# Two attention-and-feed-forward layers on one core: the quantised feed-forward's steps, the key loads and one bias moved to other places of their queues

## The chip, the cores and the metric

The kernel runs on one core of one Trainium2 chip. The core has four compute engines that each run their own queue in order: PE (matrix products), ACT (activations and copies with a scale), DVE (vector work), POOL (more vector work), and SP, a queue that only issues transfers (DMAs) between HBM and on-chip memory. Engines wait for one another by semaphores. The metric is the device time of one execution in microseconds; smaller is better.

## The reference: two layers over 32 batches

`x` is (32, 256, 256): 32 batches of 256 rows. `ctx_768` is (32, 77, 192). Each layer is an attention block and a feed-forward block, both with a residual and a layer norm on what they read:

```
x = x + L0_xattn(layernorm(x), ctx)      16 heads of 64: q = xn@Wq, k = ctx@Wk, v = ctx@Wv
x = x + L0_ffn(layernorm(x))             silu(x@wg.T) * (x@wu.T), then @wd.T, int weights / 127
x = x + L1_xattn(layernorm(x), ctx)      softmax(q k^T / 8) v @ Wo + bo
x = x + L1_ffn(layernorm(x)):
    lhs_scale = max|row| / 127 ; q_lhs = clip(round(x / lhs_scale), -127, 127)
    q_rhs the same by column of rhs ; out = (q_lhs @ q_rhs) * lhs_scale * rhs_scale
```

The feed-forward of layer 1 is thus a rounding to whole numbers, one 256 x 256 product and a scaling; that of layer 0 has three larger products.

## The kernel before

A first part computes keys and values of all batches and both layers into HBM (`keys_d`, `vals_d`) and prepares the weights. Then one long pipeline runs over h = 0 to 65: h counts batches, 0 to 31 of layer 0 and 32 to 63 of layer 1, and the last two drain. Within h there are four slots, u = 0 to 3, of four heads each, a *unit*. `lay[d]` is the layer of batch h + d, so `lay[-1] == 1` holds where the attention of batch h - 1 belongs to layer 1. Batches 4 to 28 and 36 to 60 run in hardware loops with one body each; each engine's `body` writes out, slot by slot, the order of its own queue. The order is by hand; nothing schedules it.

What a unit k = 4h + u does in its life:

- PE: `scores` (query times key) for two halves of 128 rows, t = 0 and 1, from key buffer `kb[u // 2]` (L957). One PSUM area holds them, so the scores of unit k wait for the exponentials of k - 1.
- DVE takes the maxima (L1288), ACT the exponentials with their sums (L1137), DVE the reciprocals (L1293).
- POOL makes the probabilities in three steps for each half (L1433 product, L1437 cast, L1439 low part) into one of two buffers `p16`. The cast of unit k at t = 0 waits until the transposes of unit k - 2 have landed.
- SP turns each half by a DMA transpose into `pT` (L846, `turn_probabilities`), one slot later.
- PE weighs the values three slots later (`weigh_values`, L995); ACT and DVE split the result into `oT_h` and `oT_l`; PE projects it four slots later (`project`, L980).

After the last projection of a batch, DVE forms `x1` (L1396, attention result plus `x_res`, to which POOL had added the bias, L1462). Then follow `spreads` and `moments` on DVE (L1222 to L1230), the inverse deviation `rs` by `inverse(1, ...)` on POOL (L1412), `shift` on DVE (L1235) and the normalised `x2` on ACT (L1103). In layer 1 the rounding chain follows: `am` (DVE, L1376), `lsc` and `linv` (L1281, L1284), the scaling `q_a` (ACT, L1194), `q_i` (DVE, L1328), its turn on PE (L943), the clamp `qiT` (DVE, L1360), the product (`quantised`, PE, L1016), `ya` and `yo` (DVE, L1307, L1317), and the store.

SP's queue for a batch of layer 1 holds eight transposes, two pairs of key loads, two value loads, one load of `x_res` (L894), one of the next-but-one batch's normalised input (`xn`, which is half of the tile `x_pair`, L904) and one store (L910). `load_keys(1, ...)` fills the buffer that slots 2 and 3 of the same batch read, `load_keys(0, ...)` the one that slots 0 and 1 of the next batch read. Before the change the first stands at the end of slot 0 and waits only for the last scores of the batch before:

```
if u == 0 and lay[0] is not None and like > 0:
    sp.wait_ge(s_s, QT * n)
    load_keys(1, at_own, lay[0])
```

`uses` lists in what order PE takes the two PSUM banks that the rounding, the products and the turns share.

Of the kernel before, what the change touches and what calls it, by code (L numbers as in the profile page):

```python
# [32 lines left out]
ALU = mybir.AluOpType  # L33
# [17 lines left out]
def xattn_ffn_kernel(nc, x, ctx, wq0, wk0, wv0, wo0, bo0, w_gate, w_up, w_down,  # L51
# [25 lines left out]
    with stack:  # L77
# [669 lines left out]
        def uses(lay):  # L747

            out = []
            for u in range(UNITS):  # L750
# [4 lines left out]
                if u == 1:  # L755
                    if lay[-2] == 0:
                        out.append(("turned_x2", 0))
                    if lay[1] is not None:
                        out.append(("turned_x", 0))
                    if lay[-2] == 1:  # L760
                        out.append(("turned_q", 0))
                    if lay[-2] == 0:
                        out.append(("gu", 0))
                if u == 2:
                    if lay[-3] == 0:
                        out += [("down", 0), ("down", 1)]
                    if lay[-2] == 0:
                        out.append(("gu", 1))
                    if lay[-2] == 1:
                        out += [("quant", 0), ("quant", 1)]  # L770
# [53 lines left out]
        with nc.Block() as block:  # L824

            @block.sync
            def _(sp):
# [43 lines left out]
                def body(h, like, lay, plan):  # L871
# [15 lines left out]
                    for u in range(UNITS):  # L887
                        turning = lay[(u - 1) // UNITS] is not None
                        if u == 0 and lay[-1] is not None:
# [4 lines left out]
                            sp.dma_start(x_res[:, :, :], batch_of(x_src[lay[-1]], b_res)).then_inc(s_xr, 16)  # L894
                        if turning:
# [4 lines left out]
                        if u == 2 and lay[2] == 1:  # L900
                            sp.wait_ge(s_ys, 16 * (h + 4 - B))
                            sp.sem_inc(s_ngo, 1)
                            sp.wait_ge(s_xt, h + 2)
                            sp.dma_start(xn, batch_of(n_rows, b_far)).then_inc(s_nl, 16)  # L904
                        if u == 2 and lay[1] is not None:
                            sp.wait_ge(s_s, QT * (n + 2))
                            load_keys(0, at_next, lay[1])
# [9 lines left out]
                        if turning:  # L917
                            turn_probabilities(n + u - 1, (u - 1) % UNITS, 1)
                        if u == 3 and lay[3] == 0:
                            sp.wait_ge(s_xn, QT * (h + 3))  # L920
                            sp.dma_start(x_in[:, :, :], batch_of(x_src[0], b_first)).then_inc(s_x, 16)
                        if u == 0 and lay[0] is not None and like > 0:
                            sp.wait_ge(s_s, QT * n)
                            load_keys(1, at_own, lay[0])
# [13 lines left out]
            def _(pe):  # L938
# [88 lines left out]
                def body(h, like, lay, plan):  # L1027
# [12 lines left out]
                    for u in range(UNITS):  # L1040
# [16 lines left out]
                        if u == 3 and lay[-2] == 0:  # L1057
                            gate_up(2, bank("gu", 2))
                        if lay[0] is not None:
# [9 lines left out]
                        if u == 1 and lay[-2] == 1:  # L1069
                            pe.wait_ge(s_qi, h - 1 - B)  # L1070
                            turn(as_f16(bank("turned_q", 0)), q_i).then_inc(s_qt, 1)
# [7 lines left out]
                        if u == 2 and lay[-2] == 1:  # L1079
                            pe.wait_ge(s_qe, h - 1 - B)  # L1080
                            for t in range(QT):
                                quantised(t, bank("quant", t))
                        if u == 3 and lay[-2] == 0:
                            gate_up(3, bank("gu", 3))
                        if four is not None:
                            if u == 0:
                                after(pe, s_x1, h - 1)
                            project(n + u - 4, u, four)
                        if three is not None:
# [7 lines left out]
            def _(act):  # L1097
# [15 lines left out]
                def body(h, like, lay, plan):  # L1113
# [27 lines left out]
                    for u in range(UNITS):  # L1141
# [4 lines left out]
                        if lay[-1] is not None:  # L1146
                            act.wait_ge(s_pv, n + u - 3)
                            high(oT_h[u % 2][:, :, :], OV).then_inc(s_oh, 1)
                        if u == 0 and lay[-3] == 0:
# [39 lines left out]
                        if u == 0 and lay[-2] == 1:  # L1189
                            act.wait_ge(s_li, h - 1 - B)  # L1190
                            after(act, s_qi, h - 2 - B)
                            for t in range(QT):

                                act.activation(q_a[:, t, :], x2[:, t, :], ACT.Copy, scale=linv[:, t:t + 1],  # L1194
                                               bias=MAGIC).then_inc(s_qa, 1)
# [16 lines left out]
            def _(dve):  # L1212
# [34 lines left out]
                def body(h, like, lay, plan):  # L1247
# [47 lines left out]
                    for u in range(UNITS):  # L1295
# [8 lines left out]
                        if u == 3 and lay[-2] == 1:  # L1304
                            for t in range(QT):
                                dve.wait_ge(s_a1, QT * (h - 2 - B) + t + 1)
                                dve.scalar_tensor_tensor(out=ya[:, t, :], in0=bank("quant", t)[:, 0, :],  # L1307
                                                         scalar=lsc[:, t:t + 1], in1=rhs_sb[:, :], op0=ALU.mult,
                                                         op1=ALU.mult).then_inc(s_ya, 1)
# [4 lines left out]
                        if u == 3 and lay[-2] == 1:  # L1314
                            dve.wait_ge(s_ya, QT * (h - 1 - B))
                            after(dve, s_yo, 16 * (h - 2 - B))
                            dve.tensor_tensor(yo[:, :, :], ya[:, :, :], x1[:, :, :], ALU.add).then_inc(s_ysum, 1)  # L1317
# [7 lines left out]
                        if u == 1 and lay[-2] == 1:  # L1325
                            dve.wait_ge(s_qa, QT * (h - 1 - B))
                            after(dve, s_qt, h - 2 - B)
                            dve.tensor_scalar(q_i[:, :, :], q_a[:, :, :], MAGIC + INT8_MAX, MAGIC,  # L1328
                                              ALU.min, ALU.subtract).then_inc(s_qi, 1)
# [17 lines left out]
                        if u == 0 and lay[-3] == 0:  # L1347
                            sigmoid_gate(4, h - 3)
                            hidden(4, h - 3)
# [150 lines left out]
```

## Time and profile before

| what | us |
|---|---|
| median of three runs | 1759.3 (1757.8 to 1760.6) |
| the profiled execution | 1758.15 |
| its span, first to last instruction | 1756.4 |

| engine | busy us | share of the span |
|---|---|---|
| PE | 1637.0 | 93% |
| ACT | 1373.5 | 78% |
| DVE | 1355.6 | 77% |
| POOL | 1271.7 | 72% |

The granted clock of PE was 0.987 of full speed over the span. The shares are means over three stages: the preparation to about 220 us, layer 0 to about 1090 us, layer 1 from there on. They must be read stage by stage. Busy time leaves out register work, semaphores and the issuing of DMAs, so an engine can be full with less than 100% busy, and SP has no busy time at all; its queue is read from a timeline of its issues.

### The profile page before, as it was taken

The page shows a single profiled execution, that of the slowest core. Times are in us where ns is not written, and L with a number is a line of the kernel's source. Part 1 is how long each engine was busy: PE and PEld are TensorE (multiplying, and loading weights), DVE is VectorE, ACT ScalarE, POOL GpSimd, SP SyncE. Part 2 cuts the span into 40 slices and gives each one's busy share as a digit, 9 for nine tenths or more (in the row PEclk, how much of TensorE's full clock was granted, in tenths as well). Part 3 has the DMA queues.
Part 4 walks back from the last instruction along what each step waited for, and adds up shares of the span by engine and source line. Part 5 has one row for each costly group of instructions (what it writes and reads, how often), then busy time and mean ns, then how long its engine had stood idle before and what let it go on. Part 6 is the DMA issues. An engine that isn't in the chain of part 4 may idle for free.

```text
span 1756.4 us, 56619 instructions
## 1 busy us (share of the span) xinstructions
PE 1637.0 (93%) x16300; PEld 1334.3 (76%) x16300; DVE 1355.6 (77%) x3473; ACT 1373.5 (78%) x5650; POOL 1271.7 (72%) x1920
## 2 busy tenths in 40 slices
PE   6999769999999999999999999999899999899995
PEld 3555447888888888888888888777777777777773
DVE  5666647788888888888888877777777777777774
ACT  5565558888888888888888888788888888888883
POOL 3000158888888888887888877788888888888883
PEclk9999989999999999999999999999999999999998
DMA  8677767767666666666666777898888888888893
GB/s 224 226 242 245 257 142 140 135 144 153 139 141 150 142 141 147 142 142 150 144 140 148 146 135 149 153 176 170 172 174 174 178 176 173 175 174 173 179 174 83
DMA packets 807767, 288.45 MB, mean 164 GB/s; under 512 B 686001, under 2 KB 795473, under 8 KB 807697
## 3 DMA queue, kind: packets, MB, share of 16 engines
q1 hardware_dynamic: 806432, 282.87, 73.4%
q0 software_dynamic: 1264, 4.72, 0.9%
q8 instruction: 35, 0.57, 0.1%
q14 instruction: 36, 0.29, 0.1%
HBM read 87.72 MB, written 65.54 MB: 87 GB/s over the span
## 4 chain that ended last, share of the span: by engine, by line
PE 54%; POOL 9%; SPq 8%; issue 8%; DMA 3%; DVE 3%; ACT 1%; POOLq 0%; ACTq 0%; DVEq 0%
PE psum L967 12%; PE psum L980 12%; PE psum L1003 9%; PE psum L957 8%; PE psum L995 6%; SPq L846 5%; PE psum L1010 5%; POOL pr L1433 3%; DMA kb<-keys 2%; POOL p L1439 2%; POOL p L1437 2%; PE psum L943 2%; SPq L830 2%; DVE oT_l L1214 1%; ACT ex L1137 1%
## 5 line engine op out<-in xcount | busy, mean ns | idle before, releaser
L1137 ACT ACTIVATE ex<-psum,nmax 128x77 f32<-128x77 f32 x2048 | 636.6, 332 | 69.2 <-DVE nmax L1288 65.6
L1137 ACT ACTIVATION_READ_ACCUMULATOR ex<-psum,nmax 128x1 f32 x2048 | 435.5, 213 | 0.0
L1439 POOL TENSOR_TENSOR p<-pr,p 128x308 f16<-128x308 f32 x512 | 393.8, 769 | 41.1
L1433 POOL TENSOR_TENSOR pr<-ex,rden 128x308 f32<-128x308 f32 x512 | 359.2, 702 | 40.9 <-DVE rden L1293 37.6
L1288 DVE TENSOR_REDUCE nmax<-psum 128x4 f32<-128x308 f32 x512 | 240.0, 469 | 171.4 <-PE psum L957 165.2
L1437 POOL CAST p<-pr 128x308 f16<-128x308 f32 x512 | 233.4, 456 | 105.8 <-POOL pr L1433 103.4
L980 PE MATMUL psum<-wo_h,oT_h 128*128 128x256 f16 x1024 | 280.6, 274 | 23.5 <-DVE oT_l L1214 22.9
L957 PE MATMUL psum<-kb,qT_h 128*128 128x154 f16 x2048 | 257.9, 231 | 47.9 <-DMA kb<-keys 32.6
L967 PE MATMUL psum<-xT_h,wq_h 128*128 128x256 f16 x1024 | 281.3, 275 | 1.4 <-DVE xT_l L1214 1.4
L967 PE MATMUL psum<-xT_l,wq_h 128*128 128x256 f16 x1024 | 281.4, 275 | 0.0
L967 PE MATMUL psum<-xT_h,wq_l 128*128 128x256 f16 x1024 | 281.4, 275 | 0.0
L980 PE MATMUL psum<-wo_l,oT_h 128*128 128x256 f16 x1024 | 280.3, 274 | 0.0
L980 PE MATMUL psum<-wo_h,oT_l 128*128 128x256 f16 x1024 | 280.3, 274 | 0.0
L957 PEld LDWEIGHTS psum<-kb,qT_h 128*128 128x128 f16 x2048 | 167.2, 98 | 103.4 <-issue 47.2
L957 PE MATMUL psum<-kb,qT_l 128*128 128x154 f16 x1024 | 221.4, 230 | 0.0
L995 PE MATMUL psum<-pT,vb 77*64 77x256 f16 x3072 | 217.6, 278 | 0.0
L1099 ACT ACTIVATE oT_h<-psum 128x512 f16<-128x512 f32 x256 | 154.7, 604 | 59.6 <-PE psum L995 59.5
L995 PEld LDWEIGHTS psum<-pT,vb 77*64 77x64 f16 x3072 | 148.4, 110 | 54.5 <-issue 54.1
L1214 DVE TENSOR_TENSOR oT_l<-psum,oT_h 128x512 f16<-128x512 f32 x256 | 174.7, 682 | 14.8 <-ACT oT_h L1099 14.6
L1217 DVE SCALAR_TENSOR_TENSOR qT_l<-psum,qT_h 128x512 f16<-128x512 f32 x256 | 173.7, 679 | 0.2 <-ACT qT_h L1099 0.2
L1099 ACT ACTIVATE qT_h<-psum 128x512 f16<-128x512 f32 x256 | 156.1, 610 | 3.6 <-PE psum L967 3.6
L1412 POOL TENSOR_TENSOR rs<-ve,half_neg 128x2 f32<-128x2 f32 x127 | 88.8, 699 | 74.6 <-DVE ve L1230 71.6
(162 smaller groups left out, 3760.0 us busy)
## 6 DMA issues: line engine op xcount, KB each, us to landing
keys<-ks SPq DMA_DIRECT2D x14, 1408.0 KB, 6.3
kb<-keys SPq DMA_DIRECT2D x256, 77.0 KB, 3.2
vb<-vals SPq DMA_DIRECT2D x128, 154.0 KB
vals<-vs SPq DMA_DIRECT2D x56, 256.0 KB, 2.4
x_pair<-in_x_dram SPq DMA_DIRECT2D x32, 256.0 KB, 2.7
pT<-p SPq DMA_TRANSPOSE x512, 3.2
x_res<-in_x_dram SPq DMA_DIRECT2D x32, 256.0 KB, 3.2
mid_x<-y SPq DMA_DIRECT2D x32, 256.0 KB, 2.5
```

What stands on the lines that cost most here:

```text
L957: last = pe.matmul(o, w[:, a, ts], kb[u // 2][:, part, u % 2 * PPU + a, :], start=(q == 0), stop=(q == 2))
L967: last = pe.matmul(o[:, a, :], ww[:, k, w], xx[:, k, :], start=(q == 0), stop=(q == len(terms) - 1))
L980: last = pe.matmul(OA[:, t, :], oo[:, a, ts], ww[:, m, :], start=first, stop=(u == UNITS - 1 and a == PPU - 1 and q == 2), skip_group_chec ...
L995: last = pe.matmul(OV[b * DH:(b + 1) * DH, a, :], vb[u // 2][:, part, c:c + DH], pT[u][0:NK, pp * HPU + hd, :], start=(q == 0), stop=(q == 2))
L1099: return act.activation(dst, src, ACT.Copy, scale=scale)
L1137: last = act.activation(ex[i][:, t, b, :], SC[:, t, b * NK:(b + 1) * NK], ACT.Exp, bias=nmax[i][:, t, b:b + 1], accum_out=den[i][:, t, b:b ...
L1214: return dve.tensor_tensor(dst, src, hi, ALU.subtract)
L1217: return dve.scalar_tensor_tensor(out=qT_l[i][:, :, :], in0=src, scalar=Q_DOWN, in1=qT_h[i][:, :, :], op0=ALU.mult, op1=ALU.subtract)
L1288: dve.tensor_reduce(nmax[i][:, t, :], SC[:, t, :].rearrange("p (h k) -> p h k", k=NK), AX_X, ALU.max, negate=True).then_inc(s_m, 1)
L1433: pool.tensor_tensor(pr[:, t, :, :], ex[i][:, t, :, :], r, ALU.mult).then_inc(s_p, 1)
L1437: pool.tensor_copy(d[:, t, 0, :, 0:NK], pr[:, t, :, :]).then_inc(s_ph, 1)
L1439: pool.tensor_tensor(d[:, t, 1, :, 0:NK], pr[:, t, :, :], d[:, t, 0, :, 0:NK], ALU.subtract).then_inc(s_pl, 1)
```

## The change

Order and place change; apart from one bias that another engine adds, no operation is added or left out.

- SP, both layers: `load_keys` goes ahead of the first transpose of its slot (slot 0 for buffer 1, slot 2 for buffer 0). In layer 1 the load of `xn` goes behind the second transpose of slot 2.
- POOL: for layer 1 `inverse(1, ...)` goes from the end of slot 3 to ahead of that slot's first half; for layer 0 it stays. The bias of layer 1 leaves POOL; that of layer 0 goes from the end of slot 0 to the end of slot 1.
- DVE, layer 1: the bias is added in slot 1. `am` comes ahead of the reciprocals, `q_i` behind the second maxima and ahead of `qT_l`, `qiT` behind `xT_l`, `ya` and `yo` go from the start of slot 3 to the end of slot 2.
- ACT, layer 1: `q_a` goes from the end of slot 0 behind the `oT_h` of slot 1.
- PE, layer 1: the turn of `q_i` goes behind the projection of slot 1, the quantised product ahead of the second half of the scores of slot 2.

```diff
@@ bank plan, uses() @@
+    if lay[-2] == 0:
+        out.append(("gu", 0))
     if lay[-2] == 1:
         out.append(("turned_q", 0))
-    if lay[-2] == 0:
-        out.append(("gu", 0))
 if u == 2:
     if lay[-3] == 0:
-        out += [("down", 0), ("down", 1)]
+        out.append(("down", 0))
+    if lay[-2] == 1:
+        out += [("quant", 0), ("quant", 1)]
+    if lay[-3] == 0:
+        out.append(("down", 1))
     if lay[-2] == 0:
         out.append(("gu", 1))
-    if lay[-2] == 1:
-        out += [("quant", 0), ("quant", 1)]
...
@@ SP @@
             sp.dma_start(x_res[:, :, :], batch_of(x_src[lay[-1]], b_res)).then_inc(s_xr, 16)
+        if u == 0 and lay[0] is not None and like > 0:
+            sp.wait_ge(s_s, QT * n)
+            load_keys(1, at_own, lay[0])
+        if u == 2 and lay[1] is not None:
+            sp.wait_ge(s_s, QT * (n + 2))
+            load_keys(0, at_next, lay[1])
...
             load_values(0, at_own, lay[0])
-        if u == 2 and lay[2] == 1:
...
-            sp.dma_start(xn, batch_of(n_rows, b_far)).then_inc(s_nl, 16)
-        if u == 2 and lay[1] is not None:
...
-            load_keys(0, at_next, lay[1])
...
             turn_probabilities(n + u - 1, (u - 1) % UNITS, 1)
+        if u == 2 and lay[2] == 1:
+            sp.wait_ge(s_ys, 16 * (h + 4 - B))
+            sp.sem_inc(s_ngo, 1)
+            sp.wait_ge(s_xt, h + 2)
+            sp.dma_start(xn, batch_of(n_rows, b_far)).then_inc(s_nl, 16)
...
             sp.dma_start(x_in[:, :, :], batch_of(x_src[0], b_first)).then_inc(s_x, 16)
-        if u == 0 and lay[0] is not None and like > 0:
-            sp.wait_ge(s_s, QT * n)
-            load_keys(1, at_own, lay[0])
...
@@ PE @@
             gate_up(2, bank("gu", 2))
+        if u == 2 and lay[-2] == 1:
+            pe.wait_ge(s_qe, h - 1 - B)
+            for t in range(QT):
+                quantised(t, bank("quant", t))
...
             turn(bank("turned_x", 0), xn).then_inc(s_xt, 1)
-        if u == 1 and lay[-2] == 1:
-            pe.wait_ge(s_qi, h - 1 - B)
-            turn(as_f16(bank("turned_q", 0)), q_i).then_inc(s_qt, 1)
...
             gate_up(1, bank("gu", 1))
-        if u == 2 and lay[-2] == 1:
...
-                quantised(t, bank("quant", t))
...
             project(n + u - 4, u, four)
+        if u == 1 and lay[-2] == 1:
+            pe.wait_ge(s_qi, h - 1 - B)
+            turn(as_f16(bank("turned_q", 0)), q_i).then_inc(s_qt, 1)
...
@@ ACT @@
             high(oT_h[u % 2][:, :, :], OV).then_inc(s_oh, 1)
+        if u == 1 and lay[-2] == 1:
+            act.wait_ge(s_li, h - 1 - B)
+            after(act, s_qi, h - 2 - B)
+            for t in range(QT):
+                act.activation(q_a[:, t, :], x2[:, t, :], ACT.Copy, scale=linv[:, t:t + 1],
+                               bias=MAGIC).then_inc(s_qa, 1)
...
             exponentials(n + u, u % 2, 1)
-        if u == 0 and lay[-2] == 1:
...
-                act.activation(q_a[:, t, :], x2[:, t, :], ACT.Copy, scale=linv[:, t:t + 1],
...
@@ DVE @@
             hidden(0, h - 2)
-        if u == 3 and lay[-2] == 1:
-            for t in range(QT):
-                dve.wait_ge(s_a1, QT * (h - 2 - B) + t + 1)
-                dve.scalar_tensor_tensor(out=ya[:, t, :], in0=bank("quant", t)[:, 0, :],
-                                         scalar=lsc[:, t:t + 1], in1=rhs_sb[:, :], op0=ALU.mult,
-                                         op1=ALU.mult).then_inc(s_ya, 1)
...
             hidden(1, h - 2)
-        if u == 3 and lay[-2] == 1:
-            dve.wait_ge(s_ya, QT * (h - 1 - B))
-            after(dve, s_yo, 16 * (h - 2 - B))
-            dve.tensor_tensor(yo[:, :, :], ya[:, :, :], x1[:, :, :], ALU.add).then_inc(s_ysum, 1)
...
             low(x2T_l[:, :, :], bank("turned_x2", 0), x2T_h[:, :, :]).then_inc(s_x2l, 1)
-        if u == 1 and lay[-2] == 1:
...
-            dve.tensor_scalar(q_i[:, :, :], q_a[:, :, :], MAGIC + INT8_MAX, MAGIC,
...
             hidden(4, h - 3)
+        if u == 1 and lay[-2] == 1:
+            dve.wait_ge(s_qa, QT * (h - 1 - B))
+            after(dve, s_qt, h - 2 - B)
+            dve.tensor_scalar(q_i[:, :, :], q_a[:, :, :], MAGIC + INT8_MAX, MAGIC,
+                              ALU.min, ALU.subtract).then_inc(s_qi, 1)
...
             low_q((u + 1) % 2, RG[(u + 1) % 2]).then_inc(s_ql, 1)
+        if u == 0 and lay[-2] == 1:
+            dve.wait_ge(s_x2, QT * (h - 1))
+            dve.tensor_reduce(am[:, :], x2[:, :, :], AX_X, ALU.max,
+                              apply_absolute_value=True).then_inc(s_am, 1)
+        if u == 2 and lay[-2] == 1:
+            for t in range(QT):
+                dve.wait_ge(s_a1, QT * (h - 2 - B) + t + 1)
+                dve.scalar_tensor_tensor(out=ya[:, t, :], in0=bank("quant", t)[:, 0, :],
+                                         scalar=lsc[:, t:t + 1], in1=rhs_sb[:, :], op0=ALU.mult,
+                                         op1=ALU.mult).then_inc(s_ya, 1)
...
             moments(0, st1, mv1, ve1, s_st, s_mv, h + 2)
+        if u == 1 and lay[1] is not None:
+            dve.wait_ge(s_xh, h + 2)
+            low(xT_l[:, :, :], bank("turned_x", 0), xT_h[:, :, :]).then_inc(s_xl, 1)
+        if u == 1 and lay[-1] == 1:
+            dve.wait_ge(s_xr, 16 * h)
+            bias = bo_b[lay[-1]][:, :].unsqueeze(1).to_broadcast([P, QT, D])
+            dve.tensor_tensor(x_res[:, :, :], x_res[:, :, :], bias, ALU.add).then_inc(s_xb, 1)
...
                               ALU.max).then_inc(s_qe, 1)
-        if u == 1 and lay[1] is not None:
-            dve.wait_ge(s_xh, h + 2)
-            low(xT_l[:, :, :], bank("turned_x", 0), xT_h[:, :, :]).then_inc(s_xl, 1)
...
             reciprocals(n + u, u % 2, 0)
+        if u == 2 and lay[-2] == 1:
+            dve.wait_ge(s_ya, QT * (h - 1 - B))
+            after(dve, s_yo, 16 * (h - 2 - B))
+            dve.tensor_tensor(yo[:, :, :], ya[:, :, :], x1[:, :, :], ALU.add).then_inc(s_ysum, 1)
...
             spreads(x_in, st1, s_st)
-        if u == 0 and lay[-2] == 1:
...
-            dve.tensor_reduce(am[:, :], x2[:, :, :], AX_X, ALU.max,
...
@@ POOL @@
             pool.tensor_copy(y[:, :, :], x1[:, :, :]).then_inc(s_yx, 1)
+        if u == 3 and lay[-1] == 1:
+            inverse(1, ve2, rs2, h)
         if lay[0] is not None:
             probabilities(h, u, 0)
-        if u == 0 and lay[-1] is not None:
+        if u == 1 and lay[2] == 0:
+            inverse(0, ve1, rs1, h + 2)
+        if u == 1 and lay[-1] == 0:
...
             pool.tensor_tensor(x_res[:, :, :], x_res[:, :, :], bias, ALU.add).then_inc(s_xb, 1)
-        if u == 1 and lay[2] == 0:
-            inverse(0, ve1, rs1, h + 2)
...
             inverse(2, ve3, rs3, h - 2)
-        if u == 3 and lay[-1] is not None:
+        if u == 3 and lay[-1] == 0:
...
 bodies(pool, body)

```

SP, one batch of layer 1, ahead of the second loop, before (pT_3 is the transpose of the unit of slot 3, kb1 the key buffer of slots 2 and 3):

```order
L894 DMA x_res<-mid_x 128x2x256
L846 DMA_TRANSPOSE pT_3<-p16_1 128x8x128 x2
L830 DMA kb1<-keys_1 64x8x77 x2
L846 DMA_TRANSPOSE pT_0<-p16_0 128x8x128
L837 DMA vb0<-vals_1 77x2x512
L846 DMA_TRANSPOSE pT_0<-p16_0 128x8x128
L846 DMA_TRANSPOSE pT_1<-p16_1 128x8x128
L904 DMA x_pair<-mid_n 128x2x256
L830 DMA kb0<-keys_1 64x8x77 x2
L846 DMA_TRANSPOSE pT_1<-p16_1 128x8x128
```

The same place of SP's queue now:

```order
L896 DMA x_res<-mid_x 128x2x256
L832 DMA kb1<-keys_1 64x8x77 x2
L848 DMA_TRANSPOSE pT_3<-p16_1 128x8x128 x2
L848 DMA_TRANSPOSE pT_0<-p16_0 128x8x128
L839 DMA vb0<-vals_1 77x2x512
L848 DMA_TRANSPOSE pT_0<-p16_0 128x8x128
L832 DMA kb0<-keys_1 64x8x77 x2
L848 DMA_TRANSPOSE pT_1<-p16_1 128x8x128 x2
L923 DMA x_pair<-mid_n 128x2x256
```

The keys of buffer 1 moved past two transposes, those of buffer 0 past one transpose and the load of `xn`. The instructions are the same.

POOL at the end of slot 3 in layer 1, before (p16_0 holds the unit of slot 2, p16_1 that of slot 3, rs2 is the inverse deviation for `x2`):

```order
L1433 TENSOR_TENSOR pr<-ex0,rden0 128x308
L1437 CAST p16_0<-pr 128x4x77
L1439 TENSOR_TENSOR p16_0<-pr,p16_0 128x4x77
L1433 TENSOR_TENSOR pr<-ex1,rden1 128x308
L1437 CAST p16_1<-pr 128x4x77
L1439 TENSOR_TENSOR p16_1<-pr,p16_1 128x4x77
L1412 TENSOR_TENSOR rs2<-ve2,half_neg 128x2
```

and now:

```order
L1439 TENSOR_TENSOR pr<-ex0,rden0 128x308
L1443 CAST p16_0<-pr 128x4x77
L1445 TENSOR_TENSOR p16_0<-pr,p16_0 128x4x77
L1418 TENSOR_TENSOR rs2<-ve2,half_neg 128x2
L1439 TENSOR_TENSOR pr<-ex1,rden1 128x308
L1443 CAST p16_1<-pr 128x4x77
L1445 TENSOR_TENSOR p16_1<-pr,p16_1 128x4x77
```

The inverse deviation, which waits for `ve` of a batch whose `x1` has just been formed, now stands in front of three probability steps.

DVE in slot 1 of layer 1, from the second maxima on, now (before, `q_i` and `oT_l` came ahead of these, `qiT` stood ahead of `xT_l`, and there was no bias):

```order
L1290 TENSOR_REDUCE nmax1<-psum 128x4
L1340 TENSOR_SCALAR q_i<-q_a 128x512
L1219 SCALAR_TENSOR_TENSOR qT_l0<-psum,qT_h0 128x512
L1216 TENSOR_TENSOR xT_l<-psum,xT_h 128x512
L1365 TENSOR_TENSOR x_res<-x_res,bo_b1 128x512
L1369 TENSOR_SCALAR qiT<-psum 128x512
L1295 RECIPROCAL rden1<-den1 128x4
```

The reciprocal that POOL waits for is the last of these rows.

## Rows read from the trace of the kernel before

**Rows 1.** Busy time by stage: start:end, length, then us of each engine (count), clock, DMA.
```profile
core 0: us, PE busy (x) PEld busy (x) DVE busy (x) ACT busy (x) POOL busy (x), PEclk, DMA share, GB/s
330.00:1060.00 730.00, 727.38 (x7578) 626.46 (x7577) 621.11 (x1689) 612.41 (x2562) 598.52 (x919) 1.00 0.68 144
1446.40:1466.54 20.14, 18.58 (x207) 15.64 (x205) 15.43 (x41) 17.02 (x78) 17.34 (x27) 1.00 0.86 174
```
**Rows 2.** Waits from 1330 to 1611: us in total, times, longest.
```profile
POOL p L1437 <- POOL pr L1433: 22.5, 108, 0.3
...
PE psum L957 <- DMA kb<-keys: 18.5, 14, 1.4
...
PE psum L980 <- DVE oT_l L1214: 3.4, 14, 0.3
...
POOL p L1437 <- DMA pT<-p: 1.0, 4, 0.3
```
**Rows 3.** The same stretch, waits of SP's queue.
```profile
SPq L845 <- POOL p L1439: 8.1, 14, 0.6
```
**Rows 4.** SP's timeline, issues of one batch: start, us, line, transfer, count.
```profile
1446.36 0.40 SPq L894 DMA_DIRECT2D x_res<-mid_x  x1
1447.13 2.71 SPq L846 DMA_TRANSPOSE pT<-p  x2
1450.11 1.52 SPq L830 DMA_DIRECT2D kb<-keys  x2
1451.96 1.26 SPq L846 DMA_TRANSPOSE pT<-p  x1
...
1466.54 0.40 SPq L894 DMA_DIRECT2D x_res<-mid_x  x1
```
**Rows 5.** The chain that ended last, by time: start, length, piece.
```profile
1451.02 3.10 DMA kb<-keys
...
1476.32 1.24 SPq L846
...
1491.34 3.08 DMA kb<-keys
```
**Rows 6.** PE's timeline: the scores of slot 2 and the wait ahead.
```profile
1454.35 0.30 PE L957 MATMUL psum<-kb,qT_h 128*128 128x154 f16 x2 [1.33 <-DMA kb<-keys]
```
**Rows 7.** POOL's timeline in layer 1.
```profile
1450.59 1.27 POOL L1462 TENSOR_TENSOR x_res<-x_res,bo_b 128x512 f32<-128x512 f32 x1
...
1457.09 0.44 POOL L1437 CAST p<-pr 128x308 f16<-128x308 f32 x1 [0.19 <-POOL pr L1433]
...
1459.28 0.59 POOL L1437 CAST p<-pr 128x308 f16<-128x308 f32 x1 [0.26 <-POOL pr L1433]
...
1460.94 0.70 POOL L1433 TENSOR_TENSOR pr<-ex,rden 128x308 f32<-128x308 f32 x1 [0.23 <-DVE rden L1293]
...
1462.36 0.75 POOL L1439 TENSOR_TENSOR p<-pr,p 128x308 f16<-128x308 f32 x1
...
1465.34 0.70 POOL L1412 TENSOR_TENSOR rs<-ve,half_neg 128x2 f32<-128x2 f32 x1
```
**Rows 8.** DVE's timeline in layer 1.
```profile
1458.72 0.85 DVE L1317 TENSOR_TENSOR yo<-ya,x 128x512 f32<-128x512 f32 x1
...
1464.77 0.50 DVE L1230 TENSOR_SCALAR ve<-mv 128x2 f32<-128x2 f32 x1
```
**Rows 9.** SP's timeline: issues of x_res; 25 batches, then 3, lie between.
```profile
1162.09 0.59 SPq L894 DMA_DIRECT2D x_res<-mid_x  x1
...
1667.28 0.40 SPq L894 DMA_DIRECT2D x_res<-mid_x  x1
...
1725.73 0.52 SPq L894 DMA_DIRECT2D x_res<-mid_x  x1
```
**Rows 10.** Tiles' own views: durations min/median/max; issue to landing.
```profile
L1317 DVE TENSOR_TENSOR yo<-ya,x x32: 678/851/1145, 1135.3 to 1753.0; 128x512 f32<-128x512 f32 x32
...
DMA to landing us min/median/max: 3.0/3.2/8.1
```

More of the change, by code:

```diff
@@ L899, in body @@
                             load_values(0, at_own, lay[0])
-                        if u == 2 and lay[2] == 1:
-                            sp.wait_ge(s_ys, 16 * (h + 4 - B))
-                            sp.sem_inc(s_ngo, 1)
-                            sp.wait_ge(s_xt, h + 2)
-                            sp.dma_start(xn, batch_of(n_rows, b_far)).then_inc(s_nl, 16)
-                        if u == 2 and lay[1] is not None:
-                            sp.wait_ge(s_s, QT * (n + 2))
-                            load_keys(0, at_next, lay[1])
                         if u == 3 and lay[-2] == 1:
@@ L1078, in body @@
                             gate_up(1, bank("gu", 1))
-                        if u == 2 and lay[-2] == 1:
-                            pe.wait_ge(s_qe, h - 1 - B)
-                            for t in range(QT):
-                                quantised(t, bank("quant", t))
                         if u == 3 and lay[-2] == 0:
@@ L1188, in body @@
                             exponentials(n + u, u % 2, 1)
-                        if u == 0 and lay[-2] == 1:
-                            act.wait_ge(s_li, h - 1 - B)
-                            after(act, s_qi, h - 2 - B)
-                            for t in range(QT):
-                                act.activation(q_a[:, t, :], x2[:, t, :], ACT.Copy, scale=linv[:, t:t + 1],
-                                               bias=MAGIC).then_inc(s_qa, 1)
                         if u == 0 and lay[-2] == 0:
@@ L1303, in body @@
                             hidden(0, h - 2)
-                        if u == 3 and lay[-2] == 1:
-                            for t in range(QT):
-                                dve.wait_ge(s_a1, QT * (h - 2 - B) + t + 1)
-                                dve.scalar_tensor_tensor(out=ya[:, t, :], in0=bank("quant", t)[:, 0, :],
-                                                         scalar=lsc[:, t:t + 1], in1=rhs_sb[:, :], op0=ALU.mult,
-                                                         op1=ALU.mult).then_inc(s_ya, 1)
                         if u == 3 and lay[-3] == 0:
@@ L1324, in body @@
                             low(x2T_l[:, :, :], bank("turned_x2", 0), x2T_h[:, :, :]).then_inc(s_x2l, 1)
-                        if u == 1 and lay[-2] == 1:
-                            dve.wait_ge(s_qa, QT * (h - 1 - B))
-                            after(dve, s_qt, h - 2 - B)
-                            dve.tensor_scalar(q_i[:, :, :], q_a[:, :, :], MAGIC + INT8_MAX, MAGIC,
-                                              ALU.min, ALU.subtract).then_inc(s_qi, 1)
                         if u == 2 and lay[-3] == 0:
@@ L1373, in body @@
                             spreads(x_in, st1, s_st)
-                        if u == 0 and lay[-2] == 1:
-                            dve.wait_ge(s_x2, QT * (h - 1))
-                            dve.tensor_reduce(am[:, :], x2[:, :, :], AX_X, ALU.max,
-                                              apply_absolute_value=True).then_inc(s_am, 1)
                         if u == 0 and lay[-3] == 0:
```

## The prediction

> **What bounds the kernel now.** I read the busy time by stage first, because the change sits almost wholly in layer 1. In layer 0 PE is busy 727.4 of 730 us [rows 1]: whatever moves there is behind PE's work, and only a new wait could show. In layer 1 no engine is full. A batch takes 20.14 us, in which PE is busy 18.58, POOL 17.34, ACT 17.02 and DVE 15.43 [rows 1]. PE's missing 1.56 us is two waits, once a batch each: 18.5/14 = 1.32 us for the keys and 3.4/14 = 0.24 us for `oT_l` [rows 2]. The first is the scores of slot 2, held 1.33 us [rows 6].
>
> The chain of waits says why those keys are late: it reaches a transpose on SP, runs along SP's queue for 15 us and leaves it by the key load, which lands 3.1 us after the second issue [rows 5]; the next such load is 40.3 us on, two batches. The timeline of SP gives the place: the pair of key loads is issued at 1450.11, behind two transposes that start at 1447.13 [rows 4], though the buffer was free before. The third reading decides the size of the gain: in 14 batches SP waited for anything only 8.1 us, 0.58 us a batch, always for POOL's probabilities [rows 3]. The other 20.14 - 0.58 = 19.56 us SP spends issuing: a transpose with what lies around it costs 1.5 us (two start 2.98 us before the next issue), a pair of key loads 1.85 us [rows 4]. SP is 97% occupied, more than any engine by its busy time.
>
> **The change, part by part.**
>
> *Keys of buffer 1, to the front of slot 0.* They go out at about 1447.13 instead of 1450.11, 2.98 us sooner, and land so much sooner. PE's wait of 1.33 us goes, with 1.65 us to spare. What is late next is SP itself: its instructions are the same ones in another order, so a batch cannot be shorter than SP's own 19.56 us unless an issue becomes cheaper. The two transposes of the unit of slot 3 go out 1.85 us later. Their result is weighed three slots after its scores, and in layer 1 no row shows PE waiting for `pT`. The nearer deadline is POOL's cast in slot 1, which needs the second of them landed. It goes out at about 1447.13 + 1.85 + 1.5 = 1450.5 and lands 3.2 us later [rows 10], at 1453.7; that cast follows the `pr` after the bias, some 4 us after 1450.59, and stands 1.3 us sooner once the bias is gone, at about 1453.5. So POOL may be held 0.2 us there, more if SP falls behind; it had 1.0/14 us of such waits [rows 2].
>
> *Keys of buffer 0, to the front of slot 2; `xn` behind both transposes.* The keys go out sooner by a transpose and the load of `xn`, the first transpose of slot 2 1.85 us later, and the second not later. This transpose is where SP waited for POOL, so the key load now fills that wait. I take it at nothing beside the 0.58 us already counted. `xn` is read most of a batch later.
>
> *Bias from POOL to DVE.* POOL is relieved of 1.27 us [rows 7]. Its occupation is 17.34 us plus eight pauses of 22.5/108 = 0.21 us between product and cast [rows 2], so 19.0 us at least, and at most 20.14 less its visible wait of 0.23 us [rows 7], 19.9. After the change it is 17.7 to 18.6 us. DVE gets an addition of 512 elements a row; the same form, `yo`, took 0.68 us at least and 0.85 at the median [rows 10], which brings DVE to 16.3 of 19.6 us. It stands ahead of `qiT` and of the reciprocal that POOL's next product waits for. That reciprocal comes about 0.85 us later in DVE's queue, but DVE had been idle behind it waiting for the scores that the keys held up. Nothing, then, up to 0.4 us of waiting on POOL, for which POOL has room.
>
> A row bears on the price of this for POOL: while `yo` ran from 1458.72, it took 0.85 us, not 0.68, and POOL's cast beside it 0.59 us [rows 7, 8], where another takes 0.44. The Trainium skill ("SBUF — State Buffer", section on SBUF's two separate sides) says that a vector operation with two SBUF inputs and a GpSimd operation that reads SBUF take a shared port in turns, each for its whole length. The trace agrees in kind, with about 0.15 us. By that rule the new addition can block POOL for its whole 0.68 us, and the relief is 0.59 us, not 1.27; as POOL is not the one that bounds, the sum stays as it is.
>
> *Inverse deviation ahead of the last-but-one probabilities.* POOL finishes the probabilities in front of it at 1462.36 + 0.75 = 1463.1 and `ve` ends at 1464.77 + 0.50 = 1465.3 [rows 7, 8]; `x1`, from which it comes, waits for PE. So at today's phase POOL stands 2.2 us, and three half units come later than they did. In exchange the inverse itself starts no later than at its 1465.34. At first the transposes of unit 0 would be held some 0.5 us by this. But the freed keys let PE, and with it `x1`, run ahead of SP by up to the 1.65 us found above, and then SP finds its data ready again. Price: nothing if SP bounds, the hold in full if POOL does (a rival below).
>
> *The rounding chain on ACT, DVE and PE.* The same operations. `oT_h` and `oT_l` of slot 1 no longer stand behind `q_a` and `q_i`, but PE did not wait there. The store of `yo` is not waited for in the loop. In the drain the queues are short and order means little: nothing, within 0.3 us.
>
> *Layer 0.* Keys, the bias and `inverse(0)` move under a PE that is busy all the time: nothing, within 1 us.
>
> **The sum.** From 1162.09 to 1667.28 there are 25 batches, 20.21 us each; three more to 1725.73 take 19.5 us [rows 9]. At SP's bound the 25 would take 489.0 us, 16.2 less. I take 19.65 us, for a hold now and then, so 491.3 us, 13.9 less. The last three issue less on SP and lose part of their key wait, 0.5 us each, 1.5 us. Together 15.4 us: 1758.15 - 15.4 = 1742.8 us against the profiled execution. The median of the runs lies 1.15 us above that execution, hence 1743.9; I say 1744. The bounds of a batch's length are 19.4 us (if some of SP's 19.56 was waiting that the rows don't call so), 20 us less, and 19.95 us (if half the wait comes back as another), 7 us less: 1739 to 1752 for this case.
>
> **Rivals.**
>
> *PE bounds.* If issues on SP were slow only because transfers are backed up behind them, they would get shorter and the batch fall to PE's 18.58 + 0.24 = 18.8 us: 25 x 1.4 = 35 us less, 1723. Against it: a transpose costs 1.24 us in one place of the queue and 1.26 in another [rows 4, 5]. For it: the transfer engines are busy 86% of a batch [rows 1], so something may be backed up. 7 in 100.
>
> *The wait only changes its name.* SP's 0.58 us comes back as waits for transposes, reciprocals or the inverse, each 0.2 to 0.5 us, since the ring through POOL and SP is as tight as the one through the keys: 20.1 us a batch, 1757 to 1760. For it: POOL's occupation and SP's are both near 19.6 before. Against it: POOL loses 1.27 us. 14 in 100.
>
> *POOL is held at the inverse deviation and becomes the bound.* 17.7 to 18.6 us of occupation plus the 2.2 us hold give 19.9 to 20.8, and with up to 0.68 us in which the bias on DVE blocks it 20.5 to 21.4. At 20.9 us that is 0.7 us more a batch, 25 x 0.7 = 17.5 us: 1776. It decides once hold and blocking together pass 20.14 - 18.6 = 1.5 us a batch and nothing of them is covered. Against it: being held means that POOL was ahead; it costs only if what POOL delivers afterwards is late. 13 in 100.
>
> **How the numbers follow.** The forecast has 66 in 100. Faster by over 0.2% (3.5 us, about what can be told from no change here) takes the forecast and the first rival and a little of the second, 0.74; within 0.2% is the rest of the second and a tail of the forecast, 0.12; slower is the third rival with a remainder, 0.14. The range from 1736 to 1760 holds the forecast and the second rival, 8 in 10, and leaves the first and third out.
>
> **What would show it.** In layer 1 PE's wait for `kb` is gone or under 0.3 us, x_res is issued every 19.5 to 19.8 us, SP waits for POOL under 0.2 us a batch, and POOL shows an idle stretch ahead of the inverse deviation or the cast of slot 1. In layer 0 PE stays busy over 99%. The forecast is wrong if SP still waits 0.5 us or more a batch, if POOL's gaps are short and its batch over 20 us, or if PE's busy share in layer 1 passes 97%.

## The result and the profile after

The changed kernel takes 1737.48 us (median of four runs, 1734.74 to 1740.79) against 1759.95 (four runs, 1757.80 to 1764.48): ratio 0.987, 95% interval 0.9843 to 0.9897. Its profiled execution took 1734.74 us with a span of 1733.0. One of the four runs of "all but SP's order" below took 4244.77 us, and its ratio leaves that run out.

The waits between 1330 and 1611 us answer to [rows 2] (engine and line that waited, for whom, us in total, times, longest):

```profile
POOL p L1443 <- POOL pr L1439: 21.2, 101, 0.3
...
POOL p L1443 <- DMA pT<-p: 13.5, 14, 1.2
...
PE psum L959 <- ACT ex L1139: 9.0, 10, 1.0
...
PE psum L959 <- DMA kb<-keys: 4.1, 4, 1.2
```

The wait for keys is 0.29 us a batch instead of 1.32. POOL is now held 0.96 us a batch for a transpose, and in ten places PE waits for exponentials, 0.64 us a batch, which it did not before. For SP's queue the same view, which answers to [rows 3], has no row: SP waits for nothing. Its timeline answers to [rows 4]:

```profile
1456.47 0.40 SPq L896 DMA_DIRECT2D x_res<-mid_x  x1
1457.19 1.49 SPq L832 DMA_DIRECT2D kb<-keys  x2
1459.06 4.25 SPq L848 DMA_TRANSPOSE pT<-p  x3
1463.57 0.36 SPq L839 DMA_DIRECT2D vb<-vals  x1
...
1476.07 0.40 SPq L896 DMA_DIRECT2D x_res<-mid_x  x1
```

No row stands longer than 0.8 us behind the one before. The two loads of x_res are 19.60 us apart, against 20.18 in [rows 4]. The rows between them add up to 15.6 us; the other 4.0 us lie between the rows, and the chain shows there SP's own instructions around each issue, not waits. The busy times of the stretch from 1330 to 1611 us (length, PE, PEld, DVE, ACT, POOL, clock, DMA share):

```profile
1330.00:1611.00 281.00, 266.04 (x2927) 225.32 (x2926) 232.24 (x591) 241.97 (x1105) 235.71 (x360) 1.00 0.87 179
```

PE is busy 94.7%, so it is still not the bound; in layer 0 it is busy 99.8% (728.4 of 730 us). POOL beside the bias that DVE now adds (POOL's timeline, then DVE's):

```profile
1457.55 0.71 POOL L1439 TENSOR_TENSOR pr<-ex,rden 128x308 f32<-128x308 f32 x1
...
1459.68 1.21 POOL L1439 TENSOR_TENSOR pr<-ex,rden 128x308 f32<-128x308 f32 x1
```

```profile
1459.66 0.68 DVE L1365 TENSOR_TENSOR x_res<-x_res,bo_b 128x512 f32<-128x512 f32 x1
```

The same product takes 0.71 us elsewhere and 1.21 while the addition starts beside it: POOL was relieved of 1.27 us and paid 0.50 back. It is so in each of the 15 batches from 1330 to 1611 us (1.21 or 1.22), and no other product there takes over 0.71.

Where the span's 23.4 us went, from the issue times of x_res in both traces:

| stretch | before, us | after, us | difference |
|---|---|---|---|
| start to first x_res | 252.2 | 254.5 | +2.4 |
| layer 0, to 1089 us | 837.3 | 832.6 | -4.7 |
| first three batches of layer 1 | 72.7 | 74.1 | +1.4 |
| 25 batches [rows 9] | 505.2 | 490.9 | -14.2 |
| three more | 58.4 | 56.3 | -2.2 |
| drain to the end | 30.7 | 24.6 | -6.1 |

I read nothing into the first row: over the kernels below it spreads from 253.8 to 258.9 us.

### The profile page after: what moved, and what is told of

The parts are those of the page before. It is cut to its first block, busy times and chain, and to the rows that moved or that the text cites. A ratio compares the mean times of both kernels' runs of the same rounds, so it can differ in the third digit from the quotient of the medians.

```text
span 1733.0 us, 56619 instructions
## 1 busy us (share of the span) xinstructions
PE 1629.8 (94%) x16300; PEld 1336.1 (77%) x16300; DVE 1363.6 (79%) x3505; ACT 1366.6 (79%) x5650; POOL 1233.2 (71%) x1888
## 4 chain that ended last, share of the span: by engine, by line
PE 47%; SPq 24%; issue 7%; POOL 5%; DMA 2%; DVE 2%; ACT 1%; POOLq 0%; ACTq 0%; DVEq 0%
SPq L848 15%; PE psum L969 10%; PE psum L1005 9%; PE psum L982 9%; PE psum L959 7%; PE psum L997 5%; PE psum L1012 5%; SPq L832 4%; PE psum L945 2%; POOL p L1445 2%; POOL pr L1439 1%; SPq L839 1%; POOL p L1443 1%; DMA pT<-p 1%; SPq L910 1%
## 5 line engine op out<-in xcount | busy, mean ns | idle before, releaser
L1139 ACT ACTIVATION_READ_ACCUMULATOR ex<-psum,nmax 128x1 f32 x2048 | 445.9, 218 | 0.0
L1445 POOL TENSOR_TENSOR p<-pr,p 128x308 f16<-128x308 f32 x512 | 389.6, 761 | 40.9
L1439 POOL TENSOR_TENSOR pr<-ex,rden 128x308 f32<-128x308 f32 x512 | 373.8, 730 | 36.6 <-DVE rden L1295 36.5
```

The source lines that it names most:

```text
L1139: last = act.activation(ex[i][:, t, b, :], SC[:, t, b * NK:(b + 1) * NK], ACT.Exp, bias=nmax[i][:, t, b:b + 1], accum_out=den[i][:, t, b:b ...
L1439: pool.tensor_tensor(pr[:, t, :, :], ex[i][:, t, :, :], r, ALU.mult).then_inc(s_p, 1)
L1445: pool.tensor_tensor(d[:, t, 1, :, 0:NK], pr[:, t, :, :], d[:, t, 0, :, 0:NK], ALU.subtract).then_inc(s_pl, 1)
```

## The experiments

"Batch" is the mean of the same 25 batches (x_res issues 36 to 61 of 64) in the kernel's profiled execution. "Drain" is from the last x_res to the end.

| kernel | batch, us | drain, us | median, us | ratio to before, 95% interval |
|---|---|---|---|---|
| before | 20.21 | 30.7 | 1759.95 | |
| changed | 19.64 | 24.6 | 1737.48 | 0.9843 to 0.9897 |
| SP's order alone | 19.68 | 29.6 | 1744.10 | 0.9875 to 0.9919 |
| all but SP's order | 22.40 | 27.9 | 1824.84 | 1.0325 to 1.0380 |
| bias on POOL, slot 1 | 20.07 | 24.4 | 1751.82 | 0.9919 to 0.9955 |
| bias on POOL, slot 0 | 19.63 | 28.2 | 1742.90 | 0.9878 to 0.9919 |
| rounding chain old | 19.68 | 27.1 | 1739.62 | 0.9866 to 0.9902 |
| inverse late | 19.63 | 27.9 | 1738.77 | 0.9855 to 0.9903 |
| one more store on SP | 20.41 | 25.9 | 1758.38 | 0.9974 to 0.9999 |
| changed, values on ACT | 18.82 | 27.2 | 1719.82 | 0.9741 to 0.9785 |
| SP's order, values on ACT | 19.70 | 30.6 | 1745.57 | 0.9907 to 0.9949 |
| before, values on ACT | 20.86 | 29.9 | 1794.16 | 1.0174 to 1.0222 |
| chain old, values on ACT | 19.15 | 27.7 | 1728.08 | 0.9789 to 0.9853 |
| inverse late, values on ACT | 19.35 | 30.4 | 1733.02 | 0.9816 to 0.9872 |

Each ratio is to runs of before on the same chip. My theory was that SP's issuing bounds layer 1 and that the late keys made SP wait; the main rival was that POOL's relief did it.

**SP's order alone.** The kernel before with the SP part of the diff.

> The kernel before with SP's new order alone (both key loads ahead of the first transpose of their slot, the load of xn behind the second). Theory (SP's issuing bounds layer 1, and the late keys were what made it wait): nearly the whole gain of the steady part, 19.6 to 19.8 us a batch of layer 1 instead of 20.2, that is 11 to 15 us; the drain stays as it was. Rival (POOL with the bias is as tight as SP): POOL at 19.0 to 19.9 us of occupation and held once a batch for a transpose keeps the batch at 20.0 to 20.3 us, gain under 5 us.

19.68 us a batch and no wait of SP: the numbers of the theory. Almost all of the steady gain is in the order of one queue. The drain keeps its length, 29.6 us against 30.7. But the chain of this kernel does not run along SP, as that of the changed kernel does from 1440 to 1482 us. By time:

```profile
1439.60 0.59 ACT x L1103
1440.22 0.70 DVE am L1376
...
1441.97 0.49 ACT q_a L1194
1442.46 0.49 ACT oT_h L1099
...
1459.27 0.59 ACT x L1103
```

It is a ring of one batch, 19.67 us, from `x2` through the rounding chain, `oT_h` and the projections to the next `x2`. So here two bounds lie within 0.1 us of each other, and this run alone does not tell them apart; that SP bounds rests on the changed kernel and on the two experiments that load and relieve SP in it.

**All but SP's order.** The changed kernel with SP's block of before.

> The changed kernel with SP's queue as before. Theory (the keys decide): a batch of layer 1 stays at 20.0 to 20.3 us with a PE wait for kb of about 1 us, and only the drain gains, some 5 us. Rival (POOL's relief decides): 19.6 to 19.8 us a batch, since POOL's data reach SP sooner and SP never waits; 15 us or more gained.

Both were wrong: 22.40 us a batch; the drain gains 2.8 us, not 5. The chain of this kernel, by time:

```profile
1441.08 0.71 POOL pr L1439
...
1442.56 0.76 POOL p L1445
1443.41 1.23 SPq L848
1444.92 0.69 SPq L832
1445.82 3.05 DMA kb<-keys
1449.09 0.57 PE psum L959 x6
1449.66 2.05 PE psum L969 x12
...
1456.06 1.31 PE psum L969 x12
...
1459.12 0.70 DVE x L1402
...
1463.86 0.34 issue
1464.20 0.71 POOL pr L1439
```

The ring now closes in one batch: scores of slot 2, `x1`, inverse deviation, the probabilities of slot 3 behind it, their transpose, and the keys behind that. POOL waits there for `ve` 13.2 us in 13 batches, and PE 37.9 us for keys. So the third rival of the prediction, the inverse held for `ve`, is real where the keys stand behind the transposes of slot 3; with the keys ahead of them the chain shows no such ring. No run moved the inverse alone under the old SP order, so what it costs by itself is not shown. Nor is the whole 2.19 us the ring: after the five waits for keys that no lower clock followed, the next came 21.4 to 21.5 us later, and after the seven that one followed, 23.0 to 24.2 (see the last section). The ring thus costs about 1.2 us a batch, and the clock adds the rest. The two halves of the change are not additive: alone they give -0.53 and +2.19 us a batch, together -0.57.

**Bias on POOL at the end of slot 1, and at the end of slot 0.** DVE's four lines of bias out; on POOL

```
-                        if u == 1 and lay[-1] == 0:
+                        if u == 1 and lay[-1] is not None:
```

or, in the second kernel, the same three lines under `if u == 0 and lay[-1] == 1` ahead of `inverse(0, ...)`.

> The changed kernel with the bias of layer 1 on POOL, at the end of slot 1 as in layer 0. Theory (SP bounds): POOL is 1.27 us fuller less the 0.5 us in which the bias on DVE held it, 19.3 to 20.4 us with its waits; if SP bounds with room, 19.6 us a batch and no change within 2 us. Rival (the bias had to leave): the batch grows to 20 us or more, 8 us and more lost against the changed kernel.

> The changed kernel with the bias of layer 1 on POOL at the end of slot 0, its old place. Theory (at the end of slot 1 the bias stood right behind the cast that is held for a transpose, so its 1.26 us were added to a ring of one batch; ahead of that cast it fills the hold of 0.8 us): 19.6 to 19.8 us a batch, against 20.07 with the bias at the end of slot 1. Rival (any 1.27 us on POOL costs): 20.0 us or more, as there.

At slot 1 the batch is 20.07 us, so there the rival came true and the theory failed; at slot 0 it is 19.63, the theory. The chain of the first shows why:

```profile
1450.40 1.28 SPq L848
1451.87 3.27 DMA pT<-p
1455.29 0.44 POOL p L1439
1455.98 0.54 issue
1456.52 1.26 POOL x_res L1468
1457.79 1.12 POOL pr L1435
```

The cast waits for the transpose to land, and the bias behind it is on the ring (the product behind the bias takes 1.12 us because `yo` runs beside it on DVE, 1.14 to 1.15 us in all 15 batches); ahead of the cast it fills the hold, which falls from 10.9 to 3.6 us in 14 batches. It was the place that cost 0.4 us, not the 1.27 us of work.

**One more store on SP.** `sp.dma_start(batch_of(spare_rows, b_out), yo[:, :, :])` behind the store of `yo`, to a scratch tensor.

> The changed kernel with one more store from SP in each batch of layer 1, of the same rows to a scratch tensor in HBM (256 KB). Theory (SP's issuing bounds): each batch grows by that issue with what lies around it, 0.45 to 0.62 us, to 20.1 to 20.3 us; 14 to 20 us slower over 32 batches. Rival (SP is full only because its transfers pace something else, with room of its own): 19.6 to 19.8 us and within 4 us.

20.41 us, 0.77 more a batch: each issue counts. PE waits for keys again, 24.4 us in 14 batches, and SP again waits for nothing. The 0.77 is more than the 0.62 foreseen, and SP's timeline shows where the rest is. The value load and the transpose behind the stores, in the changed kernel:

```profile
1473.41 0.34 SPq L839 DMA_DIRECT2D vb<-vals  x1
1473.97 1.31 SPq L848 DMA_TRANSPOSE pT<-p  x1
```

and behind two stores:

```profile
1486.52 0.41 SPq L841 DMA_DIRECT2D vb<-vals  x1
1487.13 1.41 SPq L850 DMA_TRANSPOSE pT<-p  x1
```

Over the batches from 1330 to 1611 us the value load takes 0.47 us there instead of 0.34 and the transpose 1.40 instead of 1.29; with 0.52 us for the store and what lies around it, that is the 0.77. So an issue is not of one fixed length; why it is longer there, no run shows.

**The changed kernel with values on ACT.** `load_values` leaves SP; on ACT, behind `oT_h`:

```
+                        if u in (1, 3) and lay[0] is not None:
+                            after(act, s_pv, n + u - 3)
+                            load_values(u // 2, at_own, lay[0])
```

> The changed kernel with the two value loads of a batch issued from ACT's queue, behind oT_h in slots 1 and 3, instead of SP's. Theory (SP's issuing bounds at 19.6 us): SP loses two issues with what lies around them, about 1.1 us a batch, so the batch falls until the next bound, PE's 18.6 to 19.0 us; 15 to 25 us faster than the changed kernel in all. Rival (the ring through POOL, DMA transposes and PE is as tight, or transfers are the limit): the batch stays at 19.4 to 19.6 us and SP waits instead. Layer 0 does not move in either.

18.82 us a batch, ratio 0.9763 to before: the fastest kernel here. PE is now all but full:

```profile
1330.00:1611.00 281.00, 276.81 (x3051) 234.37 (x3049) 243.28 (x612) 251.69 (x1151) 245.10 (x374) 1.00 0.93 187
```

98.5% of the stretch, and SP waits 0.65 us a batch (9.7 us in 15). The share alone does not prove PE the bound, since with the old rounding chain (below) PE reads 98.4% at 19.15 us a batch: the ends of its products are modelled, and a short wait may count as busy. The transfer engines are busier than in the changed kernel, 0.93 against 0.87, and move 187 GB/s against 179, so they were not what held the changed kernel.

**Values on ACT with parts of the rest undone.** SP's order alone with values on ACT; the changed kernel with the old rounding chain (`q_a`, `am`, `q_i`, `qiT`, `ya`, `yo`, the turn and the product at their old places), and with `inverse(1, ...)` for both layers at the end of slot 3, each with and without the values on ACT.

> The changed kernel with the rounding chain in its old places on ACT, DVE and PE (SP's order, the early inverse deviation and the bias on DVE stay). Theory (SP bounds the steady part, and the drain's 6 us came from the turn of q_i no longer standing ahead of a projection): 19.6 to 19.7 us a batch, the drain after the last load of x_res about 5 us longer than the changed kernel's 24.6, so 5 us slower in all. Rival (the drain's gain came from the bias having left POOL, which alone fed the last batches): the drain stays at 24.6 to 25.5 us and nothing is lost.

> The changed kernel with the inverse deviation of layer 1 back at the end of slot 3 on POOL. Theory (SP bounds, and POOL has a hold of 0.8 us to give back): 19.6 us a batch, total within 2 us of the changed kernel. Rival (the early inverse brings x2 and the rounding chain forward, and PE needs them): 19.8 us or more a batch, 4 us and more lost.

> The kernel before with SP's new order and the two value loads on ACT's queue, everything else as before. Theory (SP's queue hid what the rest of the change is worth): with 1.1 us taken off SP, POOL with the bias (19.0 to 19.9 us occupied) and the old rounding chain become the bound, and the batch stays at 19.4 to 19.7 us, against 18.8 with the whole change; 15 us or more behind that kernel. Rival (the rest of the change is worth nothing in the steady part, as it was at SP's bound): 18.8 to 19.0 us a batch.

> The changed kernel with the rounding chain in its old places on ACT, DVE and PE, and the value loads on ACT's queue. Theory (with SP freed, the bound of 19.70 us with the old rest is one ring of a batch: x1, inverse deviation, x2, am, lsc, linv, q_a, and behind it oT_h, oT_l and the projection of slot 1): q_a still stands ahead of oT_h, so the ring is only shortened by the inverse deviation coming sooner, and the batch lies between 19.2 and 19.6 us. Rival (POOL's occupation was the bound, and the bias has left it): 18.8 to 19.0 us.

> The changed kernel with the inverse deviation of layer 1 back at the end of slot 3 on POOL, and the value loads on ACT's queue. Theory (the ring through the rounding chain is opened by q_a standing behind oT_h): PE no longer waits for the chain whenever the inverse comes, 18.8 to 19.1 us a batch. Rival (the inverse deviation's place is what matters): 19.3 us or more.

With SP full, each part alone is worth nothing in the batch (19.68, 19.63). With SP freed, the whole rest is worth 0.88 us a batch (19.70 against 18.82), the chain 0.33 (19.15), the inverse's place 0.53 (19.35). The chain of SP's order with values on ACT:

```profile
1414.02 0.70 DVE x L1396
...
1417.10 0.71 POOL rs L1412
...
1419.03 0.59 ACT x L1092
1419.65 0.70 DVE am L1376
...
1421.80 0.58 ACT oT_h L1088
1422.40 0.70 DVE oT_l L1214
1423.15 1.48 PE psum L969 x12
```

The rounding chain itself is in the ring, because `q_a` stood ahead of `oT_h` in ACT's queue. It is the ring that the chain of SP's order alone already showed, and taking two issues off SP left the batch where it was, 19.70 against 19.68 us. That bears out the theory for SP's order with values on ACT. With the old chain the batch is just under my 19.2 to 19.6; with the late inverse it is over 19.1, so my claim that the chain's order alone opens the ring was wrong: there POOL takes over (its chain runs from one `rs` to the next, 19.4 us, almost wholly through POOL's probabilities). In the drain the parts with old chain and late inverse are 2.5 and 3.3 us longer than the changed kernel.

**Before with values on ACT.**

> The kernel before with nothing but the two value loads moved from SP's queue to ACT's. Theory (before the change the batch was half of a ring over two batches, 40.3 us, through the transpose of slot 2, SP's queue and the late keys): only one value load stands on SP's stretch of that ring, 0.55 us with what lies around it, so the batch falls by half of that, 0.3 us, to about 19.9 us; gain 6 to 10 us. Rival (SP's whole sum counted already before): 1.1 us less, down to 19.1 us a batch.

A miss: 20.86 us, 0.65 slower. The chain:

```profile
1402.77 0.63 SPq L830
...
1404.40 4.36 DMA pT<-p
...
1408.90 0.45 POOL p L1437
```

The second transpose of slot 2, issued behind the keys of buffer 0, lands 4.36 us after its issue, and POOL's cast of slot 3 waits for it (13.4 us in 13 batches). Keys take 4.1 us to land at the median, not 3.2; with SP's new order and values on ACT they take 3.1. A value load issued by ACT at such a time goes out beside SP's keys; that this is what delays them fits, but no run took it apart. With SP's new order alone the same move neither gains nor loses (19.70 against 19.68 us); with the whole change it gains 0.82.

## Why the prediction was right, and where it was off

- *The sum.* Against the profiled execution I was 8.0 us too high: 6.1 for the drain, 4.7 for layer 0, 0.7 and 0.3 for the batches of layer 1, less 3.8 us that the start and the first three batches of layer 1 took more. Against the median it is 6.5 us, 1744 against 1737.48. That lies in the range from 1736 to 1760, but below the 1739 to which the bounds of a batch's length led; these left out the 1.5 us of the last three batches, with which they reach from 1738 to 1751.
- *What bounds.* Right for the changed kernel. SP was occupied 19.56 us of 20.14 a batch; it now issues without a wait at 19.64 (predicted 19.65), and one more store or two fewer loads move the batch by 0.77 up and 0.82 down. What I did not see is the ring through `q_a` at 19.67 us. I priced the rounding chain at nothing because PE did not wait there; in the kernel with SP's order alone it does not show in the time either, because the two bounds lie together, but it sets the batch once SP is relieved.
- *The 25 batches.* Predicted 13.9 us less, measured 14.2. *The last three:* 1.5, measured 2.2. That a batch came within 0.01 us of 19.65 is partly luck: the 0.09 above SP's 19.56 was an allowance, not a sum.
- *The held transposes.* A hold of POOL's cast in slot 1 was foreseen at 0.2 us "more if SP falls behind". It is 0.96 us. It costs nothing by itself, but it made the bias's place matter.
- *The inverse deviation.* I foresaw a hold that PE's lead would cover. No row of the changed kernel shows POOL waiting for `ve` from 1330 to 1611 us. Undoing SP's order brought the hold out, 1.0 us a batch (13.2 in 13), in a kernel 2.2 us a batch slower than before; so the cover was the keys.
- *The bias's price on POOL.* The row of `yo` gave 0.15 us. Measured 0.50. The rule of the Trainium skill ("SBUF — State Buffer", section "SBUF: two separate sides") allowed up to the addition's whole 0.68; the trace agrees in kind and is nearer to it.
- *Layer 0 at nothing, within 1 us.* Mis-sized: 4.7 us. 2.4 of it is 0.10 us a batch over 23 batches (26.19 to 26.09). It belongs to POOL's order there, the bias behind `inverse(0, ...)`: every kernel with that order and values on SP reads 26.09 to 26.10, SP's order alone 26.21. By which wait I did not find; PE shows next to none. Another 1.3 us lies in the last five batches, 131.2 to 129.8 us, where either half of the change alone reads 129.9 to 130.0; the last 1.0 lies in the first four, where the kernels spread by 2 us.
- *The drain, nothing within 0.3 us.* This step failed: 6.1 us. From the last load of x_res to the end (busy times as above; then what PE waited for), before:

```profile
1725.73:1756.40 30.67, 12.15 (x93) 7.62 (x91) 12.39 (x27) 5.67 (x11) 4.84 (x7) 0.74 0.22 55
...
PE psum L943 <- DVE q_i L1328: 11.8, 2, 6.8
```

and changed:

```profile
1708.42:1733.00 24.58, 9.59 (x90) 6.52 (x88) 11.70 (x27) 5.37 (x11) 3.46 (x6) 0.78 0.31 68
...
PE psum L945 <- DVE q_i L1340: 6.8, 1, 6.8
```

The turn of `q_i` stood ahead of a projection and held it 5.0 us; other waits grow by 1.5, so PE waits 3.5 us less in all (14.5 to 11.0). The other 2.6 us is PE's busy time, 12.15 to 9.59 us for nearly the same number of products. The mean granted clocks, 0.74 and 0.78, come to some 16 and 11 us at the lower level (an estimate from those means), so more of the products of before ran there. Undoing the chain alone lengthens the drain by 2.5 us, not the 5 I expected, 2.2 of them as waits. With the inverse late (3.3) and the bias in slot 0 (3.6) PE waits no more than 0.4 us longer than in the changed kernel, but its products take 12.58 and 13.51 us, at a mean granted clock of 0.75 and 0.62. So those two figures are not the price of these parts, and what set the clock there no run took apart. "Order means little when queues are short" was wrong by the 3.5 us of waits; with nothing else to cover a wait, order means more.

## What to carry to other kernels

Count the issuing time of a DMA queue, with what lies between the issues, as you count an engine's, and place loads whose buffers are free early ahead of issues that wait for data. A reorder's worth depends on the rings that the other queues close. A time that fits the theory does not show the bound: look whether the chain runs there too, and test both halves of a change alone and together, and again after the present bound is removed, since parts worth nothing at one bound were worth 0.3 to 0.9 us a batch at the next. In a short stretch such as a drain, look at the clock before you give a difference to a part. Put filler work ahead of the instruction that is held, not behind it.

## What the runs showed of the hardware

- A DMA transpose of one half costs SP 1.25 to 1.28 us of issuing at the median in every kernel here, and 1.23 to 1.45 at the extremes (single issues from 1330 to 1611 us). Behind a store and a value load it took 1.29 us in the changed kernel, behind two stores and a value load 1.40.
- PE's clock fell at some of its waits. In the kernel without SP's order PE sat 2.96 us for keys, and the twelve products behind took 2.05 us, against 1.31 in the next slot [chain above: 1449.66 and 1456.06]. The row of that stretch (the last figures are clock, DMA share, GB/s):

```profile
1449.00:1454.00 5.00, 4.91 (x35) 4.04 (x36) 1.79 (x5) 1.45 (x9) 3.01 (x5) 0.66 0.90 191
1454.00:1460.00 6.00, 6.00 (x71) 4.88 (x69) 5.17 (x13) 5.01 (x27) 4.00 (x6) 1.00 0.53 96
```

  A mean of 0.66 over 5 us is a part at 1.2 GHz, the lower of the two levels, and the rest at 2.4. So that wait cost more than its length, 0.74 us on these twelve products alone. But the next batch had the same wait and kept the higher level:

```profile
1472.18 0.30 PE L959 MATMUL psum<-kb,qT_h 128*128 128x154 f16 x2 [2.93 <-DMA kb<-keys]
1472.00:1477.00 5.00, 4.82 (x54) 4.12 (x54) 3.18 (x9) 2.67 (x16) 3.13 (x6) 1.00 0.94 179
```

  Thirteen such waits of 2.83 to 2.97 us stand between 1330 and 1611 us; the clock fell at seven of them. The batch after a wait without a fall is 21.4 to 21.5 us long, with one 23.0 to 24.2. Which of the waits it falls at, no row here tells. The waits of about 1.3 us in the kernel before left it at 1.00 over the same stretch.
- A vector addition with two SBUF inputs beside a POOL product that read SBUF cost POOL 0.50 us of the addition's 0.68, in 15 batches of 15. Beside vector operations with one SBUF input or with one from PSUM the product took 0.70 us.
